# Four chained attention blocks on one core: the denominators' additions go from GpSimd to VectorE, with a new order of steps

## What is computed

```
L0: 4 heads, 4 channels each; S = q.k; softmax over the query axis; x += gamma*(Wo.o + bo)
L1: 1 head, q and k of 16 rows, v of 128; x += gamma * attention
L2: group norm of x (q) and of the 2x2 average of x (k, v: 256 positions), 8 heads of 16; x += Wproj.y
L3: group norm (32 groups), 1 head of 128; x += Wout.attention + bout
softmax(S)[n, m] = exp(S[n, m] - max) / sum of exp(S - max)
```

## Time and profile before

| | us |
|---|---|
| median of the runs | 372.79 |
| the profiled execution | 375.87 |
| its span, first to last instruction | 373.8 |
| PE busy, share | 344.5, 92% |
| DVE busy, share | 244.8, 65% |
| ACT busy, share | 191.3, 51% |
| POOL busy, share | 52.4, 14% |

### The profile page before, as it was taken

One profiled execution on the slowest core, in us unless ns is written; L12 is line 12 of the kernel. 1 busy time (PEld: TensorE's weight loads), 2 busy tenths in 40 slices (PEclk: granted clock), 3 DMA queues, 4 the chain that ended last, 5 costly groups with the idle time before them and its releaser, 6 DMA issues.

```text
span 373.8 us, 4592 instructions
## 1 busy us (share of the span) xinstructions
PE 344.5 (92%) x1766; PEld 153.3 (41%) x1766; DVE 244.8 (65%) x323; ACT 191.3 (51%) x235; POOL 52.4 (14%) x36
## 2 busy tenths in 40 slices
PE   8968998999889997889999999997999999999995
PEld 5443232344334342443343444543443344645442
DVE  1799788777876758598866336984993053691063
ACT  3634677878664267845566536145236814514220
POOL 5000000000007500000000435022200002204800
PEclk9875899999999999999999999998999999999998
DMA  8000000000000000000000000000000000000002
GB/s 303 17 0 2 0 1 3 0 2 0 2 0 2 0 0 2 2 2 2 0 4 0 2 0 0 2 0 1 2 3 2 2 0 0 2 0 2 0 10 103
DMA packets 1460, 4.43 MB, mean 12 GB/s; under 512 B 192, under 2 KB 544, under 8 KB 1312
## 3 DMA queue, kind: packets, MB, share of 16 engines
q1 hardware_dynamic: 1440, 4.15, 3.0%
HBM read 2.99 MB, written 1.05 MB: 11 GB/s over the span
## 4 chain that ended last, share of the span: by engine, by line
PE 75%; DVE 14%; ACT 6%; issue 4%; ACTq 0%; DVEq 0%
PE attn_acc L961 13%; PE attn_acc L955 11%; PE products L926 7%; PE products L930 7%; PE products L915 5%; PE products L876 5%; PE products L842 4%; PE products L846 4%; PE products L920 4%; DVE neg_max L660 3%; DVE neg_max L663 3%; DVE neg_max L666 3%; ACT probs L538 3%; PE products L854 2%; PE products L1010 2%
## 5 line engine op out<-in xcount | busy, mean ns | idle before, releaser
L538 ACT ACTIVATE probs<-products 128x1024 f32<-128x1024 f32 x128 | 126.7, 1024 | 79.4 <-PE products L936 32.2
L663 DVE TENSOR_REDUCE neg_max<-products 128x2 f32<-128x1024 f32 x64 | 75.9, 1220 | 19.7 <-PE products L876 19.6
L961 PE MATMUL attn_acc<-probs,v 128*128 128x512 f32 x128 | 62.3, 607 | 0.0
L955 PE MATMUL attn_acc<-probs,v 128*32 128x512 f32 x384 | 51.1, 612 | 0.5 <-ACT probs L538 0.5
L392 POOL TENSOR_TENSOR prob_sum<-prob_sum,probs 128x1024 f32<-128x1024 f32 x16 | 37.6, 2351 | 69.7 <-ACT probs L538 68.6
L666 DVE TENSOR_REDUCE neg_max<-products 128x1 f32<-128x1024 f32 x32 | 37.6, 1219 | 7.4 <-PE products L881 5.3
L392 POOL TENSOR_TENSOR prob_sum<-probs 128x1024 f32<-128x1024 f32 x4 | 9.4, 2354 | 231.4 <-ACT probs L538 231.4
L660 DVE TENSOR_REDUCE neg_max<-products 128x4 f32<-128x1024 f32 x32 | 37.4, 1219 | 3.7 <-PE products L889 3.6
L961 PEld LDWEIGHTS attn_acc<-probs,v 128*128 128x128 f32 x128 | 22.6, 189 | 22.7 <-issue 19.8
L930 PE MATMUL products<-rows_a,rows_b 128*128 128x512 f32 x64 | 30.6, 600 | 0.5 <-DVE neg_max L666 0.4
L392 DVE TENSOR_TENSOR prob_sum<-prob_sum,probs 128x1024 f32<-128x1024 f32 x8 | 9.8, 1222 | 19.9 <-ACT probs L538 19.7
(11 more groups left out here) (138 smaller groups left out, 387.2 us busy)
## 6 DMA issues: line engine op xcount, KB each, us to landing
w<-w_rest SPq DMA_DIRECT2D x1, 1235.5 KB, 7.4
x<-x SPq DMA_DIRECT2D x2, 512.0 KB, 4.3
tmp<-row_selector SPq DMA_DIRECT2D x1, 512.0 KB, 8.2
y<-x SPq DMA_DIRECT2D x1, 512.0 KB, 2.6
y<-x SPq DMA_DIRECT2D x2, 256.0 KB, 2.0
w<-w_first SPq DMA_DIRECT2D x1, 147.0 KB, 2.3
rounded_a<-max_rows SPq DMA_DIRECT2D x8, 4.0 KB
rows_a<-max_rows SPq DMA_DIRECT2D x4, 2.0 KB
```

The costliest lines, as they stand in the source:

```text
L538: nc.scalar.activation(P[:, n % NP, :], slot(s), ACT.Exp, scale=SCALE[L]).then_inc(read_act, 1)
L663: nc.vector.tensor_reduce(out=m[:, 2 * t:2 * t + 2], in_=slot(s).rearrange("p (a n) -> p a n", a=2), op=ALU.max, axis=AX.X, negate=True).t ...
L955: mm = nc.tensor.matmul(acc[32 * j:32 * j + 32, h], lhs, P[:, b_no[q] % NP, halves[a]], start=t0 == 0 if L == 0 else t0 % 2 == 0, stop=t0 ...
L961: mm = nc.tensor.matmul(acc[:, h], V13[b][:, t0, :], P[:, b_no[q] % NP, h], start=t0 == first, stop=t0 == last)
```

## The change

`POOL_SUM` becomes 0: no addition meets line 451's condition, and all 28 meet line 741's. GpSimd is left with the memsets of the start. The additions stand in DVE's queue at the place of their PV step. `ORDER` is another string with the same letters in the same numbers: the set of 463 steps is the same, and about three in four of the steps behind the first 28 stand at another place, nearly all by one to eight places.

```diff
-POOL_SUM = 6
+POOL_SUM = 0
 ORDER = (
-    "NNVAANANAVAAAAATAAABAABABABAABPTBAABAPBABABAPBABBA"
-    "PTAPBAPBBAAPBAPBABAPTBBPAAPBABPBABPABAPBABBPAPTBAB"
-    "PABAPBAPPVABEAEBBPBEBPBBANTNVAAPBABAPAPBABAPABTABA"
-    "PBPBABAPPABAPABBBAPPPAAAPPPABAPPPTABAPBABPPBBPPETB"
-    "PPBBEBPBPNBBNPBPBNNBPPPBAVABAPBAAPAPAEAETNEBBABAAN"
-    "BAPABBAAPANBTPAAVBABABBAPAPBBAPABEPTBBEPPPBEBBBEYP"
-    "EPPPNPNBBPPNPNBBAAPAPAAPPPPPAEPAPAVETNBBNPPBNNNBAA"
-    "PAAAPAAPVPAAPTAAPAAPBBABBAPABPTBBBPBBPBBBPBBBPEPPP"
-    "EPEYEBENPPNBBNNVAAPAPAAPAABAPPTPPEBBBBBPPBPPPBBPPP"
-    "EEPPPPPPPPEPP"
+    "NNVAAANAANAVAAATAAABAABABABABAAAPTABABAPABBPTABAPB"
+    "APPBABABPBABPABBPBABABPPATBPBABPBABPBPABABPBABVAAB"
+    "PAPTAPAAPEAEBBBEBBPAANNBVTAPABAPBABABAPAAPBPBTBABP"
+    "BABPABAPAPBAPABBAPABPAAAPPPAPPTBAAPBBPABPPBBTPPPEB"
+    "PPBBEBNPBBBNPPBNNBPBPPABAPBAPBAAPPAAEAETNVEBBABABA"
+    "BABAAPANANPTBABAPABBABAVABPPABBAEPTBBPPPEPBEBBEYEN"
+    "BPBNPPPPNNPPAAAPBPAAAPPBBAPPPPAPETPVEBNBNPBNNNVAPA"
+    "AAPPABAAAAPPTAAAPPBBBABPAABAPPTBBBPBBPBBBPBBBPPEPP"
+    "PEEBEYENPBNBPNNPPAAVAAPAABAAPPTPEBBBPPBPEPBBBBPPPP"
+    "PPPPPEPPPEPPP"
 )
```

## The result

The changed kernel takes **376.09 us** (median of 4 runs, 374.69 to 376.57), the kernel before 372.91 beside it. The ratio is 1.0079, 95% interval 1.0050 to 1.0108: slower by 3.2 us, where 370.9 was forecast. The profiled execution took 375.95, its span is 374.2.

What follows compares the result with a forecast made beforehand. The prediction took PE, busy 92% of the span, as the bound, with DVE alone setting the pace in stretches. Its terms, 0.3 + 0.4 - 2.4 + 0.7 - 0.7 - 0.2, gave -1.9 us: median 370.9, range 368.2 to 374.8.

Steps and rivals of the forecast that it cites:

- sum 1: From A0130 to A0137, four additions on DVE among eight maxima: +0.3 us (0 to +4.9).
- A21: From A2100's product to top211, three additions on DVE among 16 maxima, the tightest place: +0.4 us (0 to +3.6).
- Rival 2: Additions among back-to-back maxima make DVE the bound and pass their time to PE: 378.7 us, half 374.8; chance 0.20.
- The wait behind GpSimd: In image 1's norm chain from bcast110 to q210, the long DVE instruction goes: chain 2.06 us shorter.
- The multiplication starts at 243.5, 0.3 us earlier: Image 1's multiplication, start of the chain to q210, worked out from DVE's queue after an earlier A3000: 0.3 us gained.
- An idle time of 2.0 us stays: PE's gap before q210 shrinks only from 2.43 to 2.0 us, and the clock still falls there.
- norm 20: Before q200, PV0123 and B0133 no longer fill the chain, so PE idles more: +0.7 us (0 to +1.4).
- rival 3: The clock falls before q200 too, idle time growing from 1.51 towards 1.9 us: +1.6, 372.5 us; chance 0.13.
- Head: At the start, A0002 ahead of k01 gives DVE work in two waits: -0.7 us (0 to -1.8).
- Tail: At the end, A3100 behind two PV steps starts DVE's eight maxima earlier: -0.2 us (-0.5 to +0.5).
- I carry differences over to the median unchanged: Whole kernel: differences against the profiled 375.87 us, 3.08 above the median, were taken to hold for the median.
- rival 1: At q210 the shorter gap brings no clock fall: -1.6 us, 369.3 us; chance 0.20.

Runs made afterwards that it cites:

- new_few: The changed kernel (new order) with 20 of the 28 additions left out, none on GpSimd: 375.38 us, ratio 1.0051.
- kernels 2: The kernel before, in its old order, with all additions on DVE (POOL_SUM = 0): 381.49 us, ratio 1.0193.
- Kernel 9: The changed kernel with steps 342 to 361, from bcast110 to just ahead of A2100's group, in the old order: 378.74 us, ratio 1.0117.
- old_few: The kernel before (old order) with 20 of the 28 additions left out, none on GpSimd: 371.20 us, ratio 0.9935.

## Why the prediction was wrong, by its own steps

1. **Additions on DVE, sum 1 (+0.3) and A21 (+0.4): right, if anything too high.** After against new_few: +0.03 in 120 to 206 and 0.00 in 342 to 388, though DVE is busy 20.41 of 21 us in A21. From A2100 to top211 it is 23.76 us after and 21.20 before: the 2.6 of added PE steps and nothing else. Rival 2 (DVE the bound) didn't happen, and only because of the order (kernels 2 and 9).
2. **The wait behind GpSimd (-2.06): right**, 2.07 by old_few, and the length from bcast110 to q210 fell from 12.73 to 10.26 us, 2.47 for the 2.06 of the chain. With the rule of the Trainium skill's page "SBUF — State Buffer", section "Who interferes with whom", that the prediction names, these traces agree: without GpSimd's additions line 776 stays at 0.22 us and `max_folds` at 0.18, with them in the new order lines 776, 781 and 789 have instructions of 2.0 to 2.2 and `max_folds` one of 1.136, and no reduction from PSUM is ever longer than 1.227, with GpSimd at work or not. (The page's "does not contend" for one SBUF input holds outside VectorE's 2-port modes, a condition that the prediction leaves out.)
3. **"The multiplication starts at 243.5, 0.3 us earlier": failed.** bcast110 starts at 241.90 before and 245.32 after. A3000 did come earlier (228.43 to 227.65, although the kernel was 1.9 us late at step 296), but the window 228 to 242 shows PE busy 14.00 of 14 us: four steps of PE had moved in, and I had worked the stretch out for DVE alone. So the earlier A3000 bought nothing, 308 to 342 takes 29.76 us after and 29.73 before. The 1.1 us that were lost lie ahead of it, in 296 to 308 (11.46 for 10.35, and 11.47 in new_few), for which I had no term.
4. **"An idle time of 2.0 us stays", and nothing said of A2100: failed.** The gap before q210 is 1.22, but A2100 waits another 1.11 for `k_rows`, since v21 (0.61 us) ends before that copy where B3003 (2.3) covered it. Together 2.33, against 0.36 in old_few. This gives back 2.0 of the 2.07 gained: 342 to 388 is 40.31 us after and 40.38 before. I had priced PV30001's and B3003's move as content only, +2.6 behind A2100, and not as cover taken from in front of it. Kernel 9 shows that the cover was real: with both steps back in front, the two gaps are 0.38 and 0.
5. **norm 20 (+0.7): mis-sized**, +1.47. PE's gap before q200 is 2.09 for 1.52, nearly the 1.9 of rival 3; the one before `norm20`'s own product, which I had not looked at, is 1.56 for 0.59. Together these are 1.54 us. The clock falls as well, so rival 3's event came, with 0.13; what the fall cost by itself is not separated.
6. **28 to 206: no term, +0.60.** I priced the head and sum 1, and nothing between them, where the order differs at almost every step: +1.67 to step 120, -1.07 behind.
7. **Head (-0.7): right in sign**, -0.67, and the closeness is in part luck: profiles with the new head have 22.61 to 24.21 us from step 3 to 28, those with the old one 24.61 to 24.77. **Tail (-0.2): 0.0.**
8. **"I carry differences over to the median unchanged": failed.** The clock's fall at q210 was in the profiled execution and not in the usual one; it isn't in the changed kernel's profile either. That is rival 1's event (0.20), and it gave the median nothing, since the usual run before has no fall there. The forecast for the profiled time, 374.0, missed 375.95 by 2.0; that for the median missed by 5.2.

The measured sum is the one behind the table, +2.6, in place of -1.9. The largest single error is point 4: of the order, I priced what it did to the chain I was looking at, and let the work that it takes away from PE's waits count for nothing. Points 3 and 6 are the second: stretches whose order changed had no term, because nothing in them belonged to that chain. The difference of 4.5 us splits as 1.4 (point 3: +1.14 for -0.3, of which 1.1 is the term missing for 296 to 308), 2.0 (4), 0.8 (5), 0.6 (6), less 0.7 (1) and plus 0.2 (7); the rest, 0.2, is the small stretches.

What stays open: why the order from 28 to 120 costs 1.3 to 1.7 us, whether the 1.11 in 296 to 308 is all PE's changes between kinds of products (below), and what decides whether the clock falls at norm 20.

## To carry to other kernels

When work moves to an in-order engine and the order moves with it, price three kernels, not one: the work removed (here -2.07), the order alone, the work added in that order; the sum of parts measured in another order says nothing (10.8 us, clock falls included, and 0 for the same additions). Every step taken from in front of a waiting product is cover lost: look for the wait that it covered. And where one wait is the aim, move the one instruction that causes it: one addition of twenty moved made the kernel 0.4% faster, the whole change 0.8% slower.

## What the runs showed of the hardware that was not expected

- The same gap before the same products (2.43 and 2.44 us before q210) was followed by a clock at half in one execution and by full clock in another. In the new order the fall at norm 20 began at 148.7 us, at the end of the gap of 2.09, in one execution, and at 144.6, behind the gap of 1.56, in another that had products of zeros from 147.62 on.
- A tiny DVE instruction that ran beside a GpSimd addition of 2.35 us took 2.0 to 2.3 us instead of 0.16 to 0.22, on three lines of code (776, 781, 789); which one it met changed with the order of steps.
- Products of changing kinds ran slower than in a run of one kind. In the changed kernel's trace of PE:

```profile
215.01 1.13 PE L920 MATMUL products<-rows_a,rows_b 64*128 64x512 f32 x4
216.07 1.12 PE L961 MATMUL attn_acc<-probs,v 128*128 128x512 f32 x2
217.13 1.13 PE L920 MATMUL products<-rows_a,rows_b 64*128 64x512 f32 x4
...
218.43 3.68 PE L961 MATMUL attn_acc<-probs,v 128*128 128x512 f32 x8
222.25 1.10 PE L842 MATMUL products<-x_norm,w 128*128 128x512 f32 x2
```

A B step and a PV step take 1.06 us from start to start here, with no idle time shown, where I had 0.86 for each. These lines lie in 296 to 308, the stretch that lost 1.11 us without a wait. In the kernel before the same four PV steps took 3.43 us to the next start (214.66 to 218.09), here 3.82. No run isolates it, but 0.1 to 0.4 us at each of a few changes is the size of that loss.
